# Splitting the q, k, v products of a transformer block into fp32r parts, and moving an FP4 rounding from VectorE to ScalarE and GpSimd

## What is computed

```
h = layernorm(x) * (1 + ca) + sa                 # x: (32, 512, 256)
q, k, v = h @ Wq + bq, h @ Wk + bk, h @ Wv + bv  # 16 heads of 16
s = (q / 4) @ k.T + 8 * rel_bias[bucket]         # bias differs only near the diagonal
x = x + ga * (softmax(s) @ v @ Wo + bo)
h = layernorm(x) * (1 + cb) + sb
g, u = fp4(h) @ fp4(w_gate).T, fp4(h) @ fp4(w_up).T   # 704 columns
x = x + gb * (fp4(silu(g) * u) @ fp4(w_down).T)
```

## Time and profile before

| | before |
|---|---|
| median of 3 runs | 3264.7 us (3263.61 to 3267.48) |
| profiled execution, device time | 3262.75 us |
| its span | 3260.9 us |
| mean granted TensorE clock | 0.982 |

### The profile page before, as it was taken

The page is one execution under the profiler, slowest core; times in us unless marked ns, Lnnn a source line. Parts: engine busy times, 40 slices in busy tenths (PEclk is TensorE's granted clock), DMA queues, the critical chain, the costliest instruction groups (busy, mean ns, idle before and its releaser), DMA issues.

```text
span 3260.9 us, 67878 instructions
## 1 busy us (share of the span) xinstructions
PE 3137.3 (96%) x22404; PEld 1876.7 (58%) x22404; DVE 2765.6 (85%) x9960; ACT 2088.3 (64%) x3389; POOL 1732.0 (53%) x2104
## 2 busy tenths in 40 slices
PE   4899999999999999999999999999999999999985
PEld 1345566666656566665566665666666565666555
DVE  6678888888888888888888888888888888888865
ACT  2566666666666666666666666666666666666652
POOL 3415555555555555555555555555555555555455
PEclk7899999999999999999999999999999999999997
DMA  8344433334443324444233444332344433244000
GB/s 208 66 79 82 84 75 59 63 70 84 84 87 67 60 59 79 87 84 85 55 66 63 84 87 84 75 59 65 70 84 84 87 66 59 61 79 80 23 22 13
DMA packets 200187, 238.39 MB, mean 73 GB/s; under 512 B 23600, under 2 KB 178640, under 8 KB 199808
## 3 DMA queue, kind: packets, MB, share of 16 engines
q1 hardware_dynamic: 199840, 234.06, 37.1%
HBM read 164.57 MB, written 67.31 MB: 71 GB/s over the span
## 4 chain that ended last, share of the span: by engine, by line
PE 90%; issue 4%; DVE 3%; ACT 2%; DMA 1%; POOL 1%; SPq 0%; POOLq 0%; DVEq 0%; ACTq 0%
PE ps_x L676 25%; PE ps_o L665 15%; PE rings L647 14%; PE rings L630 14%; PE ps_x L704 6%; PE rings L633 5%; PE ps_x L711 3%; PE ps_x L722 2%; PE ps_x L743 2%; PE ps_x L735 1%; PE ps_x L728 1%; PE ps_x L697 1%; ACT probs L819 1%; DMA probs<-band_dram 0%; DVE row_max L1073 0%
## 5 line engine op out<-in xcount | busy, mean ns | idle before, releaser
L1073 DVE CUSTOM_DVE_ANT_0 rings<-rings,band_z 128x512 f32<-128x512 f32 x2048 | 1415.6, 696 | 70.5 <-issue 66.3
L819 ACT ACTIVATE probs<-rings 128x1024 f32<-128x1024 f32 x1024 | 1050.2, 1026 | 587.7 <-PE rings L633 587.5
L647 PE MATMUL rings<-k_rows,q_rows 120*128 120x512 bf16 x2048 | 790.6, 387 | 27.1 <-DVE row_max L1073 25.2
L630 PE MATMUL rings<-q_rows,k_rows 121*128 121x512 bf16 x2048 | 702.3, 383 | 12.3 <-ACT probs L819 11.2
L633 PEld LDWEIGHTS rings<-rev,band_t 128*128 128x128 f16 x5632 | 409.6, 98 | 299.9 <-issue 0.8
L665 PE MATMUL ps_o<-probs,values 128*32 128x512 f32 x4096 | 545.6, 605 | 0.0
L633 PE MATMUL rings<-rev,band_t 128*128 128x64 f16 x5632 | 500.6, 192 | 0.0
L647 PEld LDWEIGHTS rings<-k_rows,q_rows 120*128 120x128 bf16 x2048 | 197.4, 96 | 503.7 <-DVE row_max L1073 371.9
L1357 POOL TENSOR_TENSOR hidden<-hidden,inv 128x704 f32<-128x704 f32 x128 | 178.3, 1393 | 452.2 <-DVE inv L1112 452.2
L676 PE MATMUL ps_x<-w_gu_h,xq_h 128*128 128x512 f32 (+1 forms) x768 | 356.9, 465 | 1.1 <-DVE xq_l L1118 1.1
L1172 DVE SCALAR_TENSOR_TENSOR tanh<-tanh,ps_x 128x256 f32<-128x256 f32 (+1 forms) x384 | 152.3, 397 | 169.6 <-ACT tanh L929 165.3
(11 more groups left out here) (180 smaller groups left out, 6330.4 us busy)
## 6 DMA issues: line engine op xcount, KB each, us to landing
parts_dram<-parts SPq DMA_DIRECT2D x128, 384.0 KB, 2.6
q_rows<-parts_dram SPq DMA_DIRECT2D x384, 128.0 KB, 5.4
k_rows<-parts_dram SPq DMA_DIRECT2D x384, 128.0 KB, 7.9
mod_rows<-mod_rows_dram SPq DMA_DIRECT2D x32, 640.0 KB, 10.0
x_in<-in_x SPq DMA_DIRECT2D x32, 512.0 KB, 5.3
x_mid<-in_x SPq DMA_DIRECT2D x128, 128.0 KB, 2.0
out<-x_mid SPq DMA_DIRECT2D x128, 128.0 KB, 2.2
k_rows<-band_dram SPq DMA_DIRECT2D x2, 1024.0 KB, 9.5
```

What stands on the lines that cost most here:

```text
L630: mm(ps_s[:, bank, :], kr[0:ROW_MAX + 1, h, k0:k0 + P], qr[0:ROW_MAX + 1, h, :], start=True, stop=False)
L647: mm(ps_m[:, bank, :], q_rows[par][0:ROW_MAX, h, j * P:(j + 1) * P], k_rows[par][0:ROW_MAX, h, :], start=True, stop=True).then_inc(mscores ...
L819: A(prob_pair(s, j), ps_s, ACT.Exp).then_inc(exp_done, 1)
L1073: v.tensor_tensor_reduce(ps, ps, band_z[:, bias:bias + S], 1.0, LOWEST, ALU.add, ALU.max, row_max[:, par, 4 * h + j:4 * h + j + 1]).then_i ...
```

## The change

1. **q, k, v products.** Weights and h are split into high and low fp32r parts (w_qkv_h, w_qkv_l once at the start, h_h and h_l per batch), and the p and v jobs use `product`, six fp32r matmuls in place of two fp32 ones. ScalarE writes h twice (exact into x_in, rounded into h_h); GpSimd subtracts in slots 6 and 7 (h_l).
2. **q rows in three half sets** in place of two full sets. The copies of the lower heads start at slot 0 and those of the upper at slot 8; maxima stand four slots behind (MAX_LAG) in place of two; p jobs move to (8,2), (10,2), (12,2), (14,2), m1 to (4,1), m0 to (12,1), with REST_AT, MID_AT and LOW_AT accordingly.
3. **Band in f16.** It is stored as an f16 high and low part and loaded straight into band_t and hank2_half; the casts go. `band_table` runs after `weight_scales`.
4. **FP4 of the 256 columns.** ScalarE adds the constant to the square at (3,0); GpSimd adds and subtracts in place of VectorE, then scales, all ahead of L1357.
5. The memset before each reduce goes.

```diff
-    batch = {(0, 2): "v0", (2, 2): "m1", (3, 0): "v1", (4, 2): "v2", (5, 1): "xT0", (6, 2): "xT1", (7, 0): "p0",
-             (8, 2): "p1", (10, 2): "m0", (11, 0): "p2", (12, 2): "p3"}
+    batch = {(0, 2): "v0", (4, 1): "m1", (3, 0): "v1", (4, 2): "v2", (5, 1): "xT0", (6, 2): "xT1", (8, 2): "p0",
+             (10, 2): "p1", (12, 1): "m0", (12, 2): "p2", (14, 2): "p3"}
...
-REST_AT, MID_AT, LOW_AT = (8, 9, 12, 13), ((8, 3), (9, 2), (12, 3), (13, 2)), (9, 10, 13, 14)
+REST_AT, MID_AT, LOW_AT = (9, 11, 13, 15), ((9, 2), (11, 2), (13, 2), (15, 2)), (10, 12, 14, 15)
+MAX_LAG = 4
...
-        q_rows = [sb(f"q_rows{i}", [P, H, S], BF16) for i in range(2)]
+        q_half = [sb(f"q_half{i}", [P, H // 2, S], BF16) for i in range(3)]
...
-        h_t = sb("h_t", [P, DT, S])
+        h_h, h_l = sb("h_h", [P, DT, S], F32R), sb("h_l", [P, DT, S], F32R)
...
-        w_q, w_k, w_v = (sb(n, [P, DT, D]) for n in ("w_q", "w_k", "w_v"))
+        w_qkv_h, w_qkv_l = sb("w_qkv_h", [P, 3, DT, D], F32R), sb("w_qkv_l", [P, 3, DT, D], F32R)
...
-        f1_act = Steps(sem("f1_act"), "ctxT xh sq")
-        f1_dve = Steps(sem("f1_dve"), "ctxl ga res st ag amax scale inv add sub")
-        f1_pool = Steps(sem("f1_pool"), "xplus eps rstd neg shift mul add xn q")
+        f1_act = Steps(sem("f1_act"), "ctxT xh sq magic")
+        f1_dve = Steps(sem("f1_dve"), "ctxl ga res st ag amax scale inv")
+        f1_pool = Steps(sem("f1_pool"), "xplus eps rstd neg shift mul add xn radd rsub q")
...
+        def q_of(b, h):
+
+            return q_half[(2 * b + h // 8) % 3][:, h % 8, :]
+
+        def h_exact(half):
+
+            return x_in[:, 2 * half:2 * half + 2, :].rearrange("p k d -> p (k d)").rearrange("p (t q) -> p t q", t=DT)
+
+        def h_cols(h, half):
+
+            return h[:, :, 2 * half * P:(2 * half + 2) * P]
...
+            sp.dma_start(hank2_half, bass.AP(vec.tensor, vec.offset,
+                                             [[1, P], [2 * S, H], [1, 3 * HALF]])).then_inc(band_loaded, 16)
             for half in range(2):
-                sp.dma_start(hank1[HALF * half:HALF * (half + 1)],
-                             bass.AP(vec.tensor, vec.offset, [[1, HALF], [S, H], [1, 2 * P]])).then_inc(band_loaded, 16)
-            sp.dma_start(hank2, bass.AP(vec.tensor, vec.offset,
-                                        [[1, P], [S, H], [1, 3 * HALF]])).then_inc(band_loaded, 16)
+                sp.dma_start(band_t[HALF * half:HALF * (half + 1)],
+                             bass.AP(vec.tensor, vec.offset + S * half,
+                                     [[1, HALF], [2 * S, H], [1, 2 * P]])).then_inc(band_loaded, 16)
...
+            def replicate(b, half):
+
+                used = 64 * (b - 2) + 64 if half == 0 else 64 * (b - 1) + 32
+                wait(sp, scores_ready, used)
+                for op in range(2):
+                    wait(sp, parts_stored[2 * half + op], 16 * (b + 1))
+                    dst = q_half[(2 * b + half) % 3] if op == 0 else k_rows[b % 2][:, 8 * half:8 * half + 8, :]
+                    src = parts_dram[b % 2, half, op].rearrange("(h d) c n -> c d h n", d=HD)
                     for term, part in enumerate((TERMS_Q, TERMS_K)[op]):
-                        sp.dma_start(dst[16 * term:16 * term + 16, 8 * half:8 * half + 8, :],
-                                     src[part]).then_inc(replicated[half], 16)
+                        sp.dma_start(dst[16 * term:16 * term + 16], src[part]).then_inc(replicated[half], 16)
+
+            def store_parts(b, p):
+
+                after(sp, low_pool, 4 * b + p, "low")
+                wait(sp, replicated[p // 2], 16 * N_REP * (b - 1))
+                sp.dma_start(parts_dram[b % 2, p // 2, p % 2], parts[:, p % 2]).then_inc(parts_stored[p], 16)
...
+                    if s in (11, 13, 15) and it.has(2):
+                        store_parts(n + 2, (11, 13, 15).index(s))
+                    if s == 13 and n == FIRST:
+                        replicate(0, 0)
                     if s == 0 and it.has(2) and (it.steady or n > FIRST + 1):
                         load_x(n + 2)
                     if s == 0 and it.has(1):
-                        replicate(it, 1, 1)
+                        if n > FIRST + 1:
+                            replicate(n + 1, 0)
+                        store_parts(n + 1, 3)
                     if s == 0 and not it.steady and n == FIRST + 1:
                         place_consts()
+                    if s == 8 and it.has(1) and n > FIRST:
+                        replicate(n + 1, 1)
...
-                shift, h = (1, s - 2) if s >= 2 else (0, s + 14)
+                shift, h = (1, s - MAX_LAG) if s >= MAX_LAG else (0, s + 16 - MAX_LAG)
...
-                    w, half = (w_q, w_k)[p % 2], p // 2
-                    after(pe, a_act, n + 2, "h1b")
-                    for dt in range(DT):
-                        m = mm(ps[:, :], w[:, dt, half * P:(half + 1) * P], h_t[:, dt, :],
-                               start=dt == 0, stop=dt == DT - 1)
+                    half = p // 2
+                    after(pe, h_pool, n + 2, "lo1")
+                    cut = [w[:, p % 2, :, half * P:(half + 1) * P] for w in (w_qkv_h, w_qkv_l)]
+                    m = product(ps[:, :], cut, (h_h, h_l))
                 elif kind[0] == "v":
-                    after(pe, a_act, n + 1, "h1b")
+                    after(pe, h_pool, n + 1, "lo1")
                     for k in range(2 if kind == "v1" else 1):
                         tt = (0, 1, 3)[int(kind[1])] + k
-                        for dt in range(DT):
-                            m = mm(ps[:, k * D:(k + 1) * D], h_t[:, dt, tt * P:(tt + 1) * P], w_v[:, dt, :],
-                                   start=dt == 0, stop=dt == DT - 1)
+                        cut = [h[:, :, tt * P:(tt + 1) * P] for h in (h_h, h_l)]
+                        m = product(ps[:, k * D:(k + 1) * D], cut, [w[:, 2] for w in (w_qkv_h, w_qkv_l)])
...
+            A(w_qkv_h[:].rearrange("p i t n -> p (i t n)"), w_qkv_raw, ACT.Copy).then_inc(su_act, 1)
...
+                        if (r, j) == (3, 0) and it.has_tile(s, 0):
+                            after(act, f1_act, it.tile(s, 0), "sq")
+                            A(magic2[:], magic2[:], ACT.Identity, bias=floor[:]).then_inc(f1_act.sem, 1)
...
-                                for dt in range(DT):
-                                    i = A(h_t[:, dt, 2 * half * P:(2 * half + 2) * P].rearrange("p (k q) -> p k q", k=2),
+                                for o in (h_exact(half), h_cols(h_h, half)):
+                                    for dt in range(DT):
+                                        A(o[:, dt, :].rearrange("p (k q) -> p k q", k=2),
...
-                dve.wait_ge(band_loaded, 48)
-                step(v.tensor_copy(hank2_half, hank2))
-                mark("hank")
-                step(v.tensor_copy(band_t[:], hank1))
-                step(v.tensor_tensor(band_t[HALF:P], hank1[HALF:P], band_t[HALF:P], ALU.subtract))
+
+            def band_table():
...
-                v.memset(wait_pad[:, 1 + 4 * h + j:2 + 4 * h + j], 0.0)
...
-                if at == (3, 2):
-                    after(dve, f1_act, u, "sq")
-                    v.scalar_tensor_tensor(ffn_in[:], magic2[:], FLOOR, ffn_in[:], ALU.add, ALU.add).then_inc(f1_dve.sem, 1)
-                    after(dve, f1_dve, u, "add")
-                    v.scalar_tensor_tensor(ffn_in[:], magic2[:], FLOOR, ffn_in[:], ALU.add,
-                                           ALU.subtract).then_inc(f1_dve.sem, 1)
...
+            q.tensor_tensor(w_qkv_l[:].rearrange("p i t n -> p (i t n)"), w_qkv_raw,
+                            w_qkv_h[:].rearrange("p i t n -> p (i t n)").bitcast(F32), ALU.subtract).then_inc(su_pool, 1)
...
+                    if s in (6, 7) and it.has(2):
+                        half = s - 6
+                        after(pool, a_act, n + 2, f"h{half}b")
+                        q.tensor_tensor(h_cols(h_l, half), h_exact(half), h_cols(h_h, half).bitcast(F32),
+                                        ALU.subtract).then_inc(h_pool.sem, 1)
...
                     low(it, s)
+                    if r == 3 and it.has_tile(s, 0):
+                        after(pool, f1_act, u, "magic")
+                        q.tensor_tensor(ffn_in[:], ffn_in[:], magic2[:], ALU.add).then_inc(f1_pool.sem, 1)
+                        after(pool, f1_pool, u, "radd")
+                        q.tensor_tensor(ffn_in[:], magic2[:], ffn_in[:], ALU.subtract).then_inc(f1_pool.sem, 1)
+                        after(pool, f1_pool, u, "rsub")
+                        q.tensor_tensor(blocks(ffn_in[:]), blocks(ffn_in[:]), spread(scale2[:], D // BLK),
+                                        ALU.mult).then_inc(f1_pool.sem, 1)
                     if r == 3 and it.has_tile(s, 1):
                         hid = hidden[:, g % 2, :]
                         after(pool, f2_dve, it.tile(s, 1), "inv")
```

(4 more changed lines are left out.)

100 lines of the change are left out of this document (49 added, 51 removed).

## The result

The changed kernel takes 3435.74 us (median of 4 runs, 3433.78 to 3437.63) against 3266.09 us for the kernel before in the same session: 1.0524 times as long, 95% interval 1.0511 to 1.0538. The forecast of 3366 us had the direction right and missed by 70 us; the range ended at 3415. The profiled execution has a span of 3434.5 us.

What follows compares the result with a forecast made beforehand. TensorE alone was taken to bound the kernel, at 96.1 us per batch. The terms -63 + 57 + 32 + 96 - 9 - 15 + 3 = +101 us on 3262.75 gave 3364, forecast as 3366 us; range 3265 to 3415.

Steps and rivals of the forecast that it cites:

- Products, -63: 128 p jobs and 128 v tiles on TensorE get cheaper by 0.32 and 0.17 us each: 63 us saved.
- xT, +57: Slots 4 to 7: ScalarE writing h twice delays exp and hq_l; TensorE loses 1.9 us in 30 iterations: 57 us.
- p1 and p3 moved, +32: p jobs at (10,2) and (14,2) delay the next slot's exp; net 1.07 us lost, 30 times: 32 us.
- Slot 15, +96: GpSimd's p3 pass and FP4 passes delay the multiply and exp(0,0): 3.3 us lost in 29 iterations, 96 us.
- rival 3: TensorE's clock falls in the steady part, waits costing 2% of an iteration's work: +54 us, 3420 us; chance 0.04.
- Passes at nothing outside slot 15: FP4 passes ahead of the multiply in other slots with s%4 = 3 cost nothing, covered by VectorE's block scales.
- VectorE lighter, -9: 128 times two steps and 2048 memsets leave VectorE, shortening TensorE's waits for row_max: 9 us gained (0 to 25).
- Start -15: At the start, the dropped band cast and earlier weight scales let reduces begin sooner: 15 us gained (0 to 25).
- tail +3: In the tail, four or five tile groups get up to 0.7 us longer each: 3 us lost.

Runs made afterwards that it cites:

- p_old_places: Changed kernel with p3's last GpSimd pass behind the slot-15 multiply, p1 at (11,0), p3 at (15,0), p3's passes in the next iteration: 3253.35 us.
- fill_wait: Changed kernel with 20 more transposes of 128 columns on TensorE in the wait of slot 0, their result overwritten: 3408.51 us.
- low_mid: Changed kernel with GpSimd's last pass for p3 in slot 15 put between the FP4 passes and the 704-column multiply: 3341.55 us.
- before_fp4: Kernel before the change with part 4 alone (FP4 of the 256 columns by ScalarE and GpSimd, ahead of the multiply): 3287.76 us.
- after_dve_fp4: Changed kernel with the rounding of the 256 columns back on VectorE, GpSimd's scale step still ahead of the multiply: 3647.81 us.
- all_three_dve_fp4: Changed kernel, p3's last pass behind multiply, p1/p3 at (11,0)/(15,0), rounded h later, slot 7 multiply first, 256-column rounding on VectorE, scale ahead of multiply: 3438.33 us.
- after_dve_scale_last: Changed kernel with the rounding of the 256 columns back on VectorE and GpSimd's scale step behind the multiply: 3336.67 us.

## Why the forecast was right in direction and 70 us short

**Products, -63: measured -50.** The price was right for the p jobs; v jobs, in slot 0 above all, give less, and the start and the end lose some us of it.

**xT, +57: the size right, the engine that ends the wait not.** Slot 5 grew by 0.22 us (0.2 forecast). Slots 6 and 7 grew by 0.06 although a job of 1.72 us left them, so 1.78 were lost; 2.0 x 30 = 60 us. The wait is one of 1.42 us at maxima (7,1), put down to row_max behind hq_l. I had put 1.35 us at scores (7,2), on exp, and 0.3 on that reduce. exp(7,0) ends at 1548.48 and the wait at 1548.50, so either would have held TensorE. One pair less gave back 36.5 us of it; the rest came with p0's new place, as far as is known.

**p1 and p3 moved, +32: right.** In the usual iteration slots 10, 11, 14 and 15 took 21.08 us before and 23.19 after. They gained two jobs of 1.40 and lost one of 1.72 and m0, which I estimate at 0.15 from slot 12 (7.25 us before, 7.08 in p_old_places with m0 and a p job cheaper by 0.32). That leaves 1.18 us, 35 in 30 iterations. The 53 us of p_old_places compare with an arrangement that the kernel before didn't have.

**Slot 15, +96: the wait right, the step behind it missing.** This is the step that failed. TensorE waits 2.58 us for exp(0,0) where I had 2.8, through the chain that I had replayed, and I priced all that follows at full clock. The clock stood apart, as rival 3 with a chance of 0.04, priced by a mean busy share of 93% and left out of the range. The mean didn't bring the clock down; the wait did, each time, and filling it kept the clock up. Slot 0 lost 4.56 + 0.17 (v0) = 4.7 us where I had 3.3: 1.4 x 29 = 41 us, of which the clock is 33 (fill_wait) to 37 (low_mid, an estimate). With these the forecast would have been about 3400, inside its range. The Trainium skill (TensorE: Matmul & The Clock Gate, HAM oscillation) describes a loop whose idle gap lowers the clock again each time round. The rows at 1608.40 agree, at 0.54 and 0.50. The page's example waits 3 to 5 us, longer than the 2.58 here, so it couldn't have decided the case; it was reason enough to join rival 3 to my forecast's own 2.8 us wait, at 29 falls, with more than 0.04.

**Passes at nothing outside slot 15: right in steady iterations, wrong at the end.** In before_fp4 slots 3, 7 and 11 cost nothing; the 0.46 us an iteration stand in slots 15 and 0. In the last iterations, whose slots are short, it is about 1 us at a multiply. The condition I wrote for it (the cover is VectorE's block scales) was the right one, and failed there. In the kernel after, slot 12 also gives back 0.15 us without part 4.

**VectorE lighter, -9: nothing.** The waits for row_max went up from 25.2 to 98.1 us. Those waits come from reduces queued behind hq_l and ctx_l, as I had argued for most of them; the relief of part 4 alone left them at 31.4 us (before_fp4), no lower, and the memset is worth at most 0.2%.

**Start -15, measured -26; tail +3, measured +4.4.** Part 3 wasn't tried alone, so how the 26 us split isn't shown. That the start hid 11 us of the miss is luck.

Against the 70 us: slot 0 41 (the clock 33 to 37 of them), products 13, VectorE 9, xT 3, p1 and p3 3, slot 12 4, start -11, tail 1. These sum to 63. The rest fits the last slots, where before_fp4 lost 5 us ahead of its tail, and isn't assigned by a run; and the 13 isn't wholly apart from the 41, since v0 is in both.

## What to carry to other kernels

In a kernel whose engines take turns through in-order queues, replay the queue of each engine around every moved step: one GpSimd instruction, ahead of or behind another that frees a score bank two engines later, was worth 130 us, and a wrong order in an experiment of mine 311 (3647.81 against 3336.67). A relief for an engine that isn't the bound was worth nothing here, while its cost on the engine that took the work was 99 us. If TensorE must wait long once per loop, price a slow stretch behind the wait as well, as a case of the forecast itself: here it added 1.15 us to a wait of 2.58. Don't count on a length below which a wait is safe; read the granted clock behind each wait.

## What the runs showed of the hardware

A wait of TensorE can bring the clock down in an iteration in which it is busy 96.49 of 102.30 us. Each wait of 2.58 us (after) was followed, 1.3 us after work had resumed, by 3.4 us at the lower level; waits of 0.63 us (low_mid) and 1.42 us (after) left the granted clock at 1.00. In between, the length of one wait didn't decide it: in after_dve_fp4 1.91 us was followed by a fall in 23 of 25 iterations and 2.07 us in 1 of 24, and in all_three_dve_fp4 all 22 falls looked at came behind a wait of some 1.4 us with one of 0.56 close behind it. What decides there is open. At the lower level a w_o matmul of 256 columns starts every 0.21 us instead of 0.12. Filling the wait with work that nobody needs made the kernel 27 us faster. A step of VectorE on 256 columns took 1.49 us instead of 0.42 in slot 15 of after_dve_scale_last, where it ran beside GpSimd's 704-column multiply; the cause wasn't tested.
